# A two-layer graph network: the preparation of the edges in pieces, earlier due times, and an overlapped change of layers

## The chip, the cores and the metric

The kernel runs on one core of a Trainium2 chip. The metric is the device time of one execution in microseconds; three timed runs of the kernel before gave 4433.56, 4440.64 and 4442.63, so its median is 4440.64. The engines are called as in the profile: PE (matmuls), DVE (vector work), ACT (activations and copies from PSUM), POOL (GpSimd, which here does some vector work and issues every indirect DMA), SP (issues plain DMAs). PEld is PE's loading of weights.

## The reference

The input has 12,500 nodes of 128 features and 412,500 edges that are sorted by their destination. Two layers follow each other. Each normalises the nodes, applies relu, sums the neighbours' messages, and adds the result to x:

```python
h = jnp.maximum(_layernorm(x, axis=-1), 0.0)
# layer 0: Xs = h[src]; one of two weights by the edge's type; out = relu(segment_sum(msg, dst) + h @ W_self.T + b_self)
x = x + _L0_gnn_ref(h, edge_index, edge_type_2, ...)
h = jnp.maximum(_layernorm(x, axis=-1), 0.0)
# layer 1: agg = segment_sum((h @ W_in.T)[src], dst); deg = edges per node; out = agg + deg * (h @ W_out.T)
x = x + _L1_gnn_ref(h, ..., src, dst)
```

As the weights act on sums as well as on single messages, the kernel sums rows of h first and multiplies the sums by the weights afterwards.

## The kernel before

**Tiling.** The nodes make 98 blocks of 128, and a duo is two blocks. The normalised rows are kept as three bf16 pieces (384 columns together, high, middle and lowest), once in SBUF (`tab`) and once in DRAM (`tables[0]`, `tables[1]`), which is what is called the table. There are 33 edge tiles of 128 edges to a block.

**Two ways of summing.** In each layer some blocks (56 in layer 0, 38 in layer 1) are *gathered*: for each edge tile POOL fetches 128 rows of the table by an indirect DMA (line 580), five tiles make a group, the rows go into a ring of three groups, DVE makes a one-hot matrix (line 1130), and PE adds the tiles up (line 667). The other blocks (42 and 60) are *dense*: POOL fetches a list of edges (line 565) out of `pk`, a packed copy of the edges in DRAM; DVE unpacks it (line 1154), PE turns it, DVE marks rows and columns (lines 1142 and 1144), PE multiplies the marks to a part of an adjacency matrix (line 720), ACT copies it out (line 961), and PE multiplies it by all 98 blocks of `tab` (line 737, some six per step). ACT copies the sums out (line 899). In layer 0 a dense block has two such passes, one for each edge type, so there are 84 passes (60 in layer 1).

**Plan.** The class `Plan` (lines 66 to 146) gives each layer a row of steps, 16 to a dense pass: 1360 in layer 0, 976 in layer 1. Each engine's program is written out in the order of these steps. A group of gathered tiles has a due step, at which PE adds it up; the due steps spread evenly between step 8 and 12 steps ahead of the last dense pass's end. The blocks end one by one (self product, bias, relu, residual, and in layer 0 the next normalisation) as their sums become complete, at the earliest nine steps apart in layer 0 and four in layer 1. The end of a block of layer 0 stores a row of `tables[1]` (line 442, SP's queue) and one of x1.

**Between the layers.** When all 98 ends are stored, POOL starts with layer 1's lists and gathers. SP waits for the same, and then reloads `tab` from `tables[1]` in seven chunks of 14 blocks (line 461).

**Preparation.** Ahead of layer 0, x is loaded in seven chunks on SP's queue (line 406); ACT first issues eight weight and bias loads, then those of the edges: source, type, destination, and destination shifted by one tile (lines 824 to 834). Per chunk DVE takes statistics (lines 1034 to 1041), ACT computes the deviation (line 852) and DVE the scales. Then per duo ACT computes the normalised rows and their bf16 high piece (lines 862, 866), POOL subtracts (line 533, the split), ACT rounds the middle piece (line 879), and DVE makes the lowest piece (line 1053). The rings between these are four duos deep. Beside that stands the edges' work: POOL adds a flag to the source (line 522, payload) and checks the sort order, tile by tile (lines 543 and 545) and over half tiles (549 and 551), in four large operations; DVE makes keys (line 1067), payload (1063), highest and lowest node of each tile (1070, 1071), the minimum of the order checks (1074, 1080), and, behind the last duo, the windows (1087 to 1093), `far` (from 1096 on, small) and the listing of edges per block (1113 and 1115, two spans). The last of this is the flag `covered` (line 1122), on which all engines choose the fast path. PE turns the edge words for lists and indices (line 629), and ACT copies them out (`take`, line 848).

**Queues.** SP's queue then stores `pk` (lines 412 to 422) and the table's chunks (426).

## Time and profile before

| | |
|---|---|
| median of three runs | 4440.64 us |
| profiled execution | 4440.43 us |
| its span | 4438.4 us, mean granted clock 0.979 |
| PE busy | 4103.0 us, 92% |
| DVE busy | 3509.9 us, 79% |
| POOL busy | 3188.3 us, 72% |
| ACT busy | 2334.0 us, 53% |
| chain that ended last | PE 53%, POOL 24%, issue 9%, DVE 8%, ACT 3% |
| costliest groups | PE line 737: 14112 of 328 ns; POOL line 580: 3126 of 951 ns |

Shares of the whole span mix stages with different limits: the preparation, two layers and the stretch between them. The rows further down are therefore taken by stage. A row of the timeline gives start, length, engine, line, operation, tiles, shape and count, and in brackets the idle time ahead of it and what ended that. "issue" means that the engine waited for nothing that the profile shows.

### The profile page before, as it was taken

What the parts mean: (1) busy time and instruction counts of PE and PEld (TensorE: products, weight loads), DVE (VectorE), ACT (ScalarE), POOL (GpSimd) and SP (SyncE); (2) the same over time, 40 slices, a digit from 0 to 9 for tenths busy, and PEclk for the clock granted to TensorE, in tenths of its full rate; (3) what the DMA queues carried; (4) which work ended last, traced back from release to release, by engine and by line L of the source; (5) the groups of instructions that cost most, each with busy time, mean ns of one, the idle gap of its engine ahead of it and who ended that gap; (6) DMA issues with size and microseconds to landing.
All of it is one profiled execution on the core that took longest, in us unless ns stands there. A gap on an engine that the chain in (4) does not pass through costs nothing.

```text
span 4438.4 us, 102927 instructions
## 1 busy us (share of the span) xinstructions
PE 4103.0 (92%) x42000; PEld 2506.4 (56%) x42000; DVE 3509.9 (79%) x8092; ACT 2334.0 (53%) x3663; POOL 3188.3 (72%) x3360
## 2 busy tenths in 40 slices
PE   0399999999999999999999996999999999999999
PEld 0255555555555555555555554566656565656665
DVE  5678777787788778778777875888888888888886
ACT  4445555555555555555555553555555555555554
POOL 4377777777777777777777775777777777777776
PEclk9599999999999999999999998999999999999999
DMA  7223333333333333333333334433333333333332
GB/s 198 73 82 91 94 88 89 93 91 90 89 90 93 90 90 92 90 92 90 91 89 92 90 89 118 124 93 91 91 93 91 91 93 91 91 91 94 90 90 78
DMA packets 289371, 417.62 MB, mean 94 GB/s; under 512 B 70913, under 2 KB 228895, under 8 KB 288895
## 3 DMA queue, kind: packets, MB, share of 16 engines
q0 software_dynamic: 160160, 338.57, 27.1%
q1 hardware_dynamic: 121784, 66.09, 5.2%
q10 hardware_dynamic: 6951, 6.30, 0.6%
q8 instruction: 336, 5.51, 0.5%
q14 instruction: 140, 1.15, 0.1%
HBM read 373.52 MB, written 37.20 MB: 93 GB/s over the span
## 4 chain that ended last, share of the span: by engine, by line
PE 53%; POOL 24%; issue 9%; DVE 8%; ACT 3%; ACTq 1%; DMA 0%; POOLq 0%; DVEq 0%; SPq 0%
PE bank_d L737 33%; POOL arena L580 23%; PE bank_g L667 10%; PE banks_m L720 8%; DVE arena L1144 1%; POOL arena L565 1%; DVE arena L1142 1%; ACT arena L961 1%; ACT arena L899 1%; DVE arena L1130 1%; ACT arena L862 1%; ACTq L824 1%; PE bank_a L694 0%; PE bank_b L703 0%; DVE tab L1053 0%
## 5 line engine op out<-in xcount | busy, mean ns | idle before, releaser
L580 POOL DMA_INDIRECT arena<-table,idx x3126 | 2971.9, 951 | 1023.3 <-issue 924.1
L737 PE MATMUL bank_d<-tab,arena 128*128 128x384 bf16 x14112 | 2696.4, 328 | 36.1 <-ACT arena L899 35.1
L961 ACT ACTIVATE arena<-banks_m 128x784 bf16<-128x784 f32 x2304 | 1912.2, 830 | 1511.4 <-PE banks_m L720 1457.3
L737 PEld LDWEIGHTS bank_d<-tab,arena 128*128 128x128 bf16 x14112 | 1196.5, 98 | 955.3 <-issue 263.6
L1142 DVE TENSOR_TENSOR arena<-iota_ps,arena 128x256 bf16<-128x256 f32 (+1 forms) x2304 | 1220.6, 530 | 335.4 <-PE banks_m L720 302.9
L1144 DVE TENSOR_TENSOR arena<-iota_ps,arena 128x392 bf16<-128x392 f32 x2304 | 1279.4, 555 | 0.0
L720 PE MATMUL banks_m<-arena 64*128 64x98 bf16 (+1 forms) x13056 | 808.1, 226 | 49.7 <-ACT arena L961 36.3
L667 PE MATMUL bank_g<-arena 128*128 128x192 bf16 (+29 forms) x12753 | 763.2, 212 | 24.8 <-DMA arena<-table,idx 23.0
L667 PEld LDWEIGHTS bank_g<-arena 128*128 128x128 bf16 x12753 | 709.7, 97 | 118.2 <-issue 27.1
L720 PEld LDWEIGHTS banks_m<-arena 64*128 64x128 bf16 x13056 | 352.2, 95 | 580.6 <-ACT arena L961 419.8
L1130 DVE TENSOR_TENSOR arena<-iota_ps,rel 128x960 bf16<-128x960 f32 (+1 forms) x626 | 592.0, 946 | 3.2
L1183 DVE TENSOR_TENSOR d_sum<-arena 128x128 f32<-128x128 f32 x144 | 42.5, 295 | 319.3 <-ACT arena L899 307.2
L565 POOL DMA_INDIRECT arena<-pk,list_at x158 | 150.1, 950 | 108.0 <-issue 74.6
L922 ACT ACTIVATE arena<-bank_a 64x128 f32<-64x128 f32 x204 | 55.5, 272 | 150.1 <-PE bank_a L686 146.9
L931 ACT ACTIVATE arena<-bank_a 128x128 f32<-128x128 f32 x196 | 54.4, 277 | 136.3 <-PE bank_a L694 132.7
L899 ACT ACTIVATE arena<-bank_d 128x384 f32<-128x384 f32 x144 | 70.8, 491 | 58.1 <-PE bank_d L737 58.1
L533 POOL TENSOR_TENSOR arena<-arena,tab 128x256 f32<-128x256 f32 x49 | 35.4, 726 | 80.5 <-ACT tab L866 75.6
L685 PE MATMUL bank_a<-ident,arena 128*128 128x128 f32 x102 | 30.4, 298 | 65.8 <-DVE arena L1177 65.8
L1201 DVE SCALAR_TENSOR_TENSOR arena<-bias,count,bank_b 128x128 f32<-128x128 f32 x98 | 33.8, 345 | 61.2 <-issue 56.7
L629 PE MATMUL banks_m<-ident,arena 128*128 128x128 f32 x30 | 6.8, 397 | 78.8 <-ACT arena L848 39.5
L1154 DVE SCALAR_TENSOR_TENSOR arena<-arena,node 128x192 f32<-128x192 int32 x158 | 64.8, 410 | 16.0 <-DMA arena<-pk,list_at 16.0
L694 PE MATMUL bank_a<-ident_b,tab 128*128 128x128 bf16 x588 | 65.0, 219 | 5.1 <-ACT arena L908 2.2
(133 smaller groups left out, 1594.6 us busy)
## 6 DMA issues: line engine op xcount, KB each, us to landing
arena<-table,idx POOLq DMA_INDIRECT x3126
table<-tab SPq DMA_DIRECT2D x7, 1344.0 KB, 5.6
table<-arena SPq DMA_DIRECT2D x98, 96.0 KB
tab<-table SPq DMA_DIRECT2D x7, 1344.0 KB, 17.1
x<-arena SPq DMA_DIRECT2D x98, 64.0 KB
arena<-x SPq DMA_DIRECT2D x98, 64.0 KB
arena<-in_x_dram SPq DMA_DIRECT2D x97, 64.0 KB
out_dram<-arena SPq DMA_DIRECT2D x97, 64.0 KB
```

The source lines that it names most:

```text
L565: pool.indirect_dma_start(out=pack[:, i % PACKS, :], out_offset=None, in_=pk, in_offset=bass.IndirectOffsetOnAxis(ap=list_at[:, m:m + 1], ...
L580: pool.indirect_dma_start(out=rows[:, g % RINGS * GROUP + t % GROUP, :], out_offset=None, in_=tables[l], in_offset=bass.IndirectOffsetOnAx ...
L667: last = pe.matmul(bank_g[p % 2][:, to:to + (c1 - c0) * y], rows[:, at, a * F:(a + 1) * F], hot[:, at, c0 * y:c1 * y], start=(a == 0 and p ...
L694: last = pe.matmul(bank_a[:, 0:P], mine[:, a * F:(a + 1) * F], ident_b[:, :], start=(a == 0), stop=(a == 2))
L720: last = pe.matmul(bank_m[hf][:, n * nc_:(n + 1) * nc_], is_row[at, s_ % MARKS, n, :], is_col[at, s_ % MARKS, n * nc_:(n + 1) * nc_], star ...
L737: last = pe.matmul(bank_d[:, 0:RW], adj[q % 2][:, b * P:(b + 1) * P], tab[:, b, :], start=(b == 0), stop=(b == NB - 1))
L899: act.activation(d_sb[:, :], bank_d[:, 0:RW], ACT.Copy).then_inc(s.dense_out, 1)
L961: act.activation((adj0, adj1)[l][q % 2].rearrange("p c (h d) -> p c h d", h=2)[:, :, :, n * j:n * j + n], banks_m[:, :, 0:n * nc_].rearran ...
L1130: dve.tensor_tensor(hot[:, at:at + n, 0:c], iota_w[:, 0:c].unsqueeze(1).to_broadcast([P, n, c]), (rel0, rel1)[l][:, ts[0]:ts[0] + n].unsqu ...
L1142: dve.tensor_tensor(is_row[:, s_ % MARKS, 0:n, :], iota_r.unsqueeze(1).to_broadcast([P, n, P]), rc[:, i % 2, 0, pr:pr + n].unsqueeze(2).to ...
L1144: dve.tensor_tensor(is_col[:, s_ % MARKS, 0:n * nc_].rearrange("p (n c) -> p n c", n=n), iota_c[l].unsqueeze(1).to_broadcast([P, n, nc_]), ...
L1154: after(dve.scalar_tensor_tensor(out=arena[:, V_AT:E_AT], in0=pack[:, k, 0:W3].bitcast(i32), scalar=node[:, m:m + 1], in1=pack[:, k, W3:2 ...
```

## The change

- The edge loads are issued by SP, between the third and the fourth chunk of x, in the order destination, type, shifted destination, source. ACT issues only the weights and biases.
- POOL's payload and its two order checks are cut into 39 pieces of two of the 26 columns, 65 instructions. They stand between the splits of duos 7 to 34, one or two pieces ahead of each.
- DVE's edge work goes into a table `jobs`: for a chunk of lowest pieces, jobs in its middle and at its end. Behind the last duo remain `far` and the second span of the listing. The payload on DVE now comes ahead of POOL's flag.
- PE's centre product comes first, ACT's copy of the indices a chunk later.
- Layer 0's table rows are reloaded by chunks: `early` holds chunks 0, 1, 2, 4 and 5, which SP reloads inside layer 0's row of ends, as soon as the blocks are stored and the last dense pass is past the chunk (`s_passed`). Chunks 3 and 6 are reloaded where all were.
- POOL fetches layer 1's first four lists before it waits for the stores.
- The due steps end 28 steps ahead of the last pass's end, where it was 12, in both layers.

```diff
-            self.due = [8 + g * (self.S - 12) // self.groups for g in range(self.groups)]
+            self.due = [8 + g * (self.S - 28) // self.groups for g in range(self.groups)]
...
+    early = {}
+    for c in range(XCH):
+        passed = 16 * plans[0].Q + -(-XB[c + 1] * 16 // NB)
+        ended = max(q for q, (step, m) in enumerate(plans[0].end) if step + 9 <= passed)
+        if all(plans[0].seq[m] <= ended for m in range(XB[c], XB[c + 1])):
+            early[c] = ended
...
+            def load_x(c):
                 n0, n1 = XB[c], min(XB[c + 1], NB - 1)
                 sp.dma_start(tab_x[:, n0:n1, 0:F],
                              x[n0 * P:n1 * P, :].rearrange("(n p) f -> p n f", p=P)).then_inc(s_x[c], 16)
+            def load_edges(a, lst):
+                sp.dma_start(raw_i[a][:, 0:FCH * P].rearrange("p (c e) -> p c e", e=P),
+                             lst[0:FCH * P * P].rearrange("(c p e) -> p c e", p=P, e=P)).then_inc(s_edges[a], 16)
+                sp.dma_start(raw_i[a][0:XTRA, FCH * P:FCH * P + P],
+                             lst[FCH * P * P:FULL * P].rearrange("(p e) -> p e", e=P)).then_inc(s_edges[a], 16)
+                if REM:
+                    sp.dma_start(raw_i[a][XTRA:XTRA + 1, FCH * P:FCH * P + REM],
+                                 lst[FULL * P:E].rearrange("(p e) -> p e", p=1)).then_inc(s_edges[a], 16)
+            for c in range(3):
+                load_x(c)
+            sp.wait_ge(s_pads, 4)
+            load_edges(0, dst)
+            load_edges(1, etype)
...
+            load_edges(2, src)
+            for c in range(3, XCH):
+                load_x(c)
...
+            def reload(c):
+                sp.dma_start(tab[:, XB[c]:XB[c + 1], :],
...
+                    for c in early:
+                        if l == 0 and early[c] == q:
+                            for k in range(2):
+                                sp.wait_ge(s_stored[0][k], 32 * ((q + 2 - k) // 2))
+                            sp.wait_ge(s_passed, list(early).index(c) + 1)
+                            reload(c)
...
-            pool.wait_ge(s_edges[2], PIECES)
-            pool.tensor_scalar(raw[2], raw_i[2], float(VALID), None, op0=ALU.add).then_inc(s_pay, 1)
...
+            def piece(i):
+                a, b = i % PCS * 2, min(i % PCS * 2 + 2, CH)
+                if i < PCS:
+                    if i == 0:
+                        pool.wait_ge(s_edges[0], PIECES)
+                        pool.wait_ge(s_edges[3], PIECES)
+                    pool.tensor_tensor(steps[:, a:b, 0:P - 1], dst_i[:, a:b, 1:P], dst_i[:, a:b, 0:P - 1],
+                                       op=ALU.subtract).then_inc(s_order, 1)
+                    pool.tensor_tensor(steps[:, a:b, P - 1], nxt_t[:, a:b, 0], dst_i[:, a:b, P - 1],
+                                       op=ALU.subtract).then_inc(s_order, 1)
+                elif i < 2 * PCS:
+                    if i == PCS:
+                        pool.wait_ge(s_pay, 1)
+                    pool.tensor_scalar(pay_t[:, a:b, :], pay_t[:, a:b, :], float(VALID), None, op0=ALU.add).then_inc(s_pay, 1)
+                else:
+                    if i == 2 * PCS:
+                        pool.wait_ge(s_order, 2 * PCS + 1)
+                    pool.tensor_tensor(steps[:, a:b, 0:HALF], dst_i[:, a:b, HALF:P], dst_i[:, a:b, 0:HALF],
+                                       op=ALU.subtract).then_inc(s_order, 1)
+                    pool.tensor_tensor(steps[:, a:b, HALF:P], nxt_t[:, a:b, :], dst_i[:, a:b, HALF:P],
+                                       op=ALU.subtract).then_inc(s_order, 1)
-                if d == DUOS // 7:
-                    pool.wait_ge(s_edges[0], PIECES)
-                    pool.wait_ge(s_edges[3], PIECES)
-                    pool.tensor_tensor(steps[:, :, 0:P - 1], dst_i[:, :, 1:P], dst_i[:, :, 0:P - 1],
-                                       op=ALU.subtract).then_inc(s_order, 1)
-                    pool.tensor_tensor(steps[:, :, P - 1], nxt_t[:, :, 0], dst_i[:, :, P - 1],
-                                       op=ALU.subtract).then_inc(s_order, 1)
-                if d == DUOS * 3 // 7:
-                    pool.wait_ge(s_order, 3)
-                    pool.tensor_tensor(steps[:, :, 0:HALF], dst_i[:, :, HALF:P], dst_i[:, :, 0:HALF],
-                                       op=ALU.subtract).then_inc(s_order, 1)
-                    pool.tensor_tensor(steps[:, :, HALF:P], nxt_t[:, :, :], dst_i[:, :, HALF:P],
-                                       op=ALU.subtract).then_inc(s_order, 1)
+                while i < 3 * PCS and (i + 1) * (XB[5] // 2 - XB[1] // 2) <= 3 * PCS * (d + 1 - XB[1] // 2):
+                    piece(i)
+                    i += 1
                 split(d)
...
+                    pool.wait_ge(L[0].unpacked, len(plans[0].fetch))
+                    while n < PACKS:
+                        fetch(n)
+                        n += 1
...
+                    if l == 0 and q == plan.Q - 1 and any(XB[c + 1] == b + 1 for c in early):
+                        last.then_inc(s_passed, 1)
...
+            jobs = {1: ((payload,), (keys,)), 2: ((highest_of_tiles,), (lowest_of_tiles, order)), 4: ((), (order_half,)),
+                    5: ((windows,), (windows_1,)), 6: ((lambda: listing(0),), ())}
             def lowest(c):
-                for d in range(XB[c] // 2, XB[c + 1] // 2):
+                d0, d1 = XB[c] // 2, XB[c + 1] // 2
+                for d in range(d0, d1):
                     dve.wait_ge(s_mid, d + 1)
                     dve.tensor_tensor(tab[:, 2 * d:2 * d + 2, 2 * F:3 * F], rest[:, d % RING, :, :],
                                       tab[:, 2 * d:2 * d + 2, F:2 * F], op=ALU.subtract).then_inc(s_low, 1)
-
-            tiles = raw_i[0].rearrange("p (c e) -> p c e", e=P)
-            steps = lr[:, 0:CP].bitcast(i32)
+                    if c in jobs and d == (d0 + d1) // 2 - 1:
+                        for job in jobs[c][0]:
+                            job()
+                if c in jobs:
+                    for job in jobs[c][1]:
+                        job()
...
                 statistics(c)
-                if c == 0:
-                    dve.wait_ge(s_edges[1], PIECES)
-                    dve.wait_ge(s_pay, 1)
-                    after(dve.scalar_tensor_tensor(out=raw[2], in0=raw_i[1], scalar=float(TYPED), in1=raw[2],
-                                                   op0=ALU.mult, op1=ALU.add), s_pay, 2)
-                if c == 1:
-                    dve.wait_ge(s_edges[0], PIECES)
-                    dve.scalar_tensor_tensor(out=raw[1], in0=raw_i[0], scalar=2.0, in1=raw_i[1],
-                                             op0=ALU.mult, op1=ALU.add).then_inc(s_v, 1)
-                if c == 2:
-                    dve.tensor_reduce(tmax[:, :], tiles, axis=AX.X, op=ALU.max).then_inc(s_extent, 1)
-                    dve.tensor_reduce(tmin[:, :], tiles, axis=AX.X, op=ALU.min).then_inc(s_extent, 1)
-                if c == 3:
-                    dve.wait_ge(s_order, 2)
-                    after(dve.tensor_reduce(worst[:, 0:1], steps, axis=AX.X, op=ALU.min), s_order, 3)
                 scales(c)
                 if c > 0:
                     lowest(c - 1)
-                if c == 4:
-                    dve.wait_ge(s_order, 5)
-                    after(dve.tensor_reduce(worst[:, 1:2], steps, axis=AX.X, op=ALU.min), s_order, 6)
-                    dve.memset(lr[:, 0:BEFORE], -1.0).then_inc(s_before, 1)
-                    if LRW > BEFORE + CP:
-                        dve.memset(lr[:, BEFORE + CP:LRW], float(PAD_NODE)).then_inc(s_before, 1)
             lowest(XCH - 1)
```

POOL in the preparation, before: the splits of line 533 wait for ACT's high pieces and DVE's lowest ones, and four large checks stand between them.

```order
L533 TENSOR_TENSOR arena<-arena,tab 128x256 [waits s_hi] x4
L533 TENSOR_TENSOR arena<-arena,tab 128x256 [waits s_low,s_hi] x3
L543 TENSOR_TENSOR arena<-arena 128x26x127 [waits s_edges_next,s_edges_dst]
L545 TENSOR_TENSOR arena<-arena 128x26
L533 TENSOR_TENSOR arena<-arena,tab 128x256 [waits s_low,s_hi] x14
L549 TENSOR_TENSOR arena<-arena 128x26x64 [waits s_order]
L551 TENSOR_TENSOR arena<-arena 128x26x64
L533 TENSOR_TENSOR arena<-arena,tab 128x256 [waits s_low,s_hi] x28
```

The same place now; line 576 is the split, lines 591 and 593 the first check.

```order
L576 TENSOR_TENSOR arena<-arena,tab 128x256 [waits s_low,s_hi] x3
L591 TENSOR_TENSOR arena<-arena 128x2x127 [waits s_edges_next,s_edges_dst]
L593 TENSOR_TENSOR arena<-arena 128x2
L576 TENSOR_TENSOR arena<-arena,tab 128x256 [waits s_low,s_hi]
L591 TENSOR_TENSOR arena<-arena 128x2x127
L593 TENSOR_TENSOR arena<-arena 128x2
```

Each large operation became thirteen small ones, which stand between single splits.

POOL at the start of layer 1, before: line 565 fetches a list, line 580 gathers a tile, and `s_stored00` and `s_stored01` count layer 0's stores.

```order
L393 COMPARE_AND_BRANCH
L565 DMA arena<-pk,list_at 128x384 [waits s_stored01,s_stored00]
L565 DMA arena<-pk,list_at 128x384
L580 DMA arena<-table,idx 128x384 x15
L565 DMA arena<-pk,list_at 128x384
L580 DMA arena<-table,idx 128x384 [waits l1_added]
```

The same place now; line 625 fetches a list, line 644 gathers a tile.

```order
L404 COMPARE_AND_BRANCH
L625 DMA arena<-pk,list_at 128x384 [waits l0_unpacked]
L625 DMA arena<-pk,list_at 128x384 x3
L644 DMA arena<-table,idx 128x384 [waits s_stored01,s_stored00]
L644 DMA arena<-table,idx 128x384 x14
L644 DMA arena<-table,idx 128x384 [waits l1_added]
```

Four list fetches moved ahead of the wait for the stores, and wait for the unpacking of layer 0's last lists in its place.

PE at the end of layer 1, before: line 667 adds gathered tiles, the one with x3 being the last; line 737 is the dense product, six to a step; lines 694, 707 and 708 belong to the end of a block.

```order
L667 MATMUL bank_g<-arena 128x6 x3
L737 MATMUL bank_d<-tab,arena 128x384 x25
L667 MATMUL bank_g<-arena 128x2 x3
L737 MATMUL bank_d<-tab,arena 128x384 x12
L694 MATMUL bank_a<-ident_b,tab 128x128 x3
L737 MATMUL bank_d<-tab,arena 128x384 x6
L707 MATMUL bank_b<-wT,arena 128x128
L708 MATMUL bank_b<-wT,arena 128x128
L737 MATMUL bank_d<-tab,arena 128x384 x18
```

The same place now, from the last gathered tile on: line 731 adds gathered tiles, line 784 builds the adjacency, line 801 is the dense product, lines 758, 771 and 772 belong to ends.

```order
L801 MATMUL bank_d<-tab,arena 128x384 x7
L731 MATMUL bank_g<-arena 128x2 x3
L784 MATMUL banks_m<-arena 128x98 x8
L801 MATMUL bank_d<-tab,arena 128x384 x6
L784 MATMUL banks_m<-arena 128x98 x8
L801 MATMUL bank_d<-tab,arena 128x384 x6
L758 MATMUL bank_a<-ident_b,tab 128x128 x3
L784 MATMUL banks_m<-arena 128x98 x8
L801 MATMUL bank_d<-tab,arena 128x384 x6
```

Behind the last gathered tile there stood 49 dense products and no build; now the builds and 147 dense products of one and a half passes stand there.

## Rows read from the trace of the kernel before

**Rows 1.** Windows of layer 0 and of layer 1
```profile
190.93:2731.76 2540.83, 2450.71 (x22244) 1469.24 (x22244) 2001.54 (x4996) 1343.74 (x2101) 1862.85 (x1958) 0.99 0.32 90
2788.46:4438.40 1649.94, 1601.49 (x19391) 993.32 (x19389) 1359.09 (x2794) 883.41 (x1297) 1232.31 (x1298) 1.00 0.32 91
```

**Rows 2.** Chain of waits from 3000 to 3300 us, its shares by line
```profile
by line: POOL arena L580 72.8%; issue 24.3%; POOL arena L565 3.2%
```

**Rows 3.** Waits in layer 1, POOL 2760 to 3000, PE 3000 to 4300 us
```profile
POOL arena L580 <- PE bank_g L667: 4.8, 4, 2.9
PE bank_g L667 <- DMA arena<-table,idx: 20.0, 35, 1.5
```

**Rows 4.** Waits in layer 0, 300 to 2300 us
```profile
POOL arena L580 <- PE bank_g L667: 74.5, 68, 4.0
```

**Rows 5.** Timeline of the loads and of ACT's deviations
```profile
0.98 37.35 SPq L406 DMA_DIRECT2D tab<-in_x_dram  x7
12.79 1.30 PE L618 MATMUL bank_g<-ident,arena 128*128 128x128 f32 x5 [12.79 <-DMA bias<-in_L_gnn_b_self_dram]
33.88 8.33 ACTq L831 DMA_DIRECT2D arena<-in_dst_dram  x1
44.78 0.30 ACT L852 ACTIVATE arena<-arena,cells 128x14 f32<-128x14 f32 x1
49.77 0.30 ACT L852 ACTIVATE arena<-arena,cells 128x14 f32<-128x14 f32 x1 [1.55 <-DVE arena L1041]
124.20 0.30 ACT L852 ACTIVATE arena<-arena,cells 128x14 f32<-128x14 f32 x1 [4.75 <-DVE arena L1041]
139.59 0.31 ACT L852 ACTIVATE arena<-arena,cells 128x14 f32<-128x14 f32 x1 [4.43 <-DVE arena L1041]
```

**Rows 6.** Timeline, one lowest piece and one split
```profile
57.72 0.69 DVE L1053 TENSOR_TENSOR tab<-arena,tab 128x256 bf16<-128x256 f32 x1 [0.84 <-ACT tab L879]
86.70 0.67 POOL L533 TENSOR_TENSOR arena<-arena,tab 128x256 f32<-128x256 f32 x1 [5.58 <-ACT tab L866]
```

**Rows 7.** Timeline of DVE's tail behind the last duo
```profile
164.73 0.99 DVE L1087 TENSOR_SCALAR arena<-arena 128x3234 int16<-128x3234 int16 x1
172.63 1.84 DVE L1093 TENSOR_SCALAR idx<-idx 128x3234 int32<-128x3234 int32 x1
182.85 2.71 DVE L1113 TENSOR_TENSOR arena<-arena,node 128x2450 f32<-128x2450 f32 x1
188.93 0.15 DVE L1122 TENSOR_SCALAR covered<-bank_b 1x1 int32<-1x1 f32 x1
```

**Rows 8.** Timeline of the payload, the order checks and their neighbours
```profile
20.60 8.65 POOL L522 TENSOR_SCALAR arena<-arena 128x3328 f32<-128x3328 int32 x1 [16.36 <-DMA arena<-in_src_dram]
58.09 5.87 POOL L543 TENSOR_TENSOR arena<-arena 128x3302 int32<-128x3302 int32 x1
59.25 5.41 DVE L1053 TENSOR_TENSOR tab<-arena,tab 128x256 bf16<-128x256 f32 x2 [0.84 <-ACT tab L879]
93.42 3.88 POOL L549 TENSOR_TENSOR arena<-arena 128x1664 int32<-128x1664 int32 x1
```

**Rows 9.** Windows, a stretch with stores on SP's queue
```profile
50.00:55.00 5.00, 1.56 (x8) 1.56 (x9) 4.93 (x5) 4.91 (x15) 3.20 (x3) 1.00 1.20 314
```

**Rows 10.** Timeline between the layers
```profile
2740.50 0.35 SPq L442 DMA_DIRECT2D table<-arena  x1
2747.08 0.33 SPq L442 DMA_DIRECT2D table<-arena  x1
2750.47 0.95 POOL L565 DMA_INDIRECT arena<-pk,list_at  x1 [33.41 <-DMA x<-arena]
2758.02 0.42 DVE L1154 SCALAR_TENSOR_TENSOR arena<-arena,node 128x192 f32<-128x192 int32 x1 [10.96 <-DMA arena<-pk,list_at]
```

**Rows 11.** Timeline of the end of layer 1
```profile
4401.30 0.64 PE L667 MATMUL bank_g<-arena 128*128 128x78 bf16 x15
4416.24 0.95 POOL L580 DMA_INDIRECT arena<-table,idx  x1 [0.30 <-issue]
```

More of the change, by code:

```diff
@@ L59, in gnn_kernel @@
     XCH = 7
+    PCS = -(-CH // 2)
     XB = [NB * c // XCH // 2 * 2 if c < XCH else NB for c in range(XCH + 1)]
@@ L403, in _ @@
             sp.wait_ge(s_x_pad, 1)
-            for c in range(XCH):
+            def load_x(c):
                 n0, n1 = XB[c], min(XB[c + 1], NB - 1)
@@ L1048, in scales, with keys, payload @@
                                                op0=ALU.mult, op1=ALU.mult), s_shift, 2 * c + 2)
+            tiles = raw_i[0].rearrange("p (c e) -> p c e", e=P)
+            steps = lr[:, 0:CP].bitcast(i32)
+            GR = -(-CH // 4)
+            def keys():
+                dve.wait_ge(s_edges[0], PIECES)
+                dve.scalar_tensor_tensor(out=raw[1], in0=raw_i[0], scalar=2.0, in1=raw_i[1],
+                                         op0=ALU.mult, op1=ALU.add).then_inc(s_v, 1)
+            def payload():
+                dve.wait_ge(s_edges[1], PIECES)
+                dve.wait_ge(s_edges[2], PIECES)
+                after(dve.scalar_tensor_tensor(out=raw[2], in0=raw_i[1], scalar=float(TYPED), in1=raw_i[2],
+                                               op0=ALU.mult, op1=ALU.add), s_pay, 1)
@@ new lines, in listing @@
+            def listing(k):
+                a, n = SPANS[k]
+                if k == 0:
+                    dve.wait_ge(s_trc, 2 + 3 * GR)
+                    dve.wait_ge(s_packed, 16 * 6)
+                seen = lr[:, a:a + NB * TPB].rearrange("p (m t) -> p m t", t=TPB)[:, :, 0:n]
+                less = raw[0][:, 0:NB * TPB].rearrange("p (m t) -> p m t", t=TPB)[:, :, 0:n]
+                after(dve.tensor_tensor(less, seen, node[:, :].unsqueeze(2).to_broadcast([P, NB, n]), op=ALU.is_lt),
+                      s_lists, 2 * k + 1)
+                after(dve.tensor_reduce(before[:, k, :], less, axis=AX.X, op=ALU.add), s_lists, 2 * k + 2)
@@ L1106, in _ @@
                                      op0=ALU.is_lt, op1=ALU.add).then_inc(s_missed, 1)
[L1108 to L1115 removed]
+            for k in range(1, len(SPANS)):
+                listing(k)
             for k in range(1, len(SPANS)):
```

86 lines of the change are left out of this document (43 added, 43 removed).

## The prediction

> **What bounds the kernel now.** I read the share of each engine first, then the windows of the two layers, then the chain of waits, then the timeline of the three places that the change touches.
>
> Layer 0 takes 2541 us and layer 1 1650 us from its first dense matmul on [rows 1]; ahead of the one stand 191 us of preparation, between them lie 57. The reader is to see that PE is busy 96 to 97% of both layers, which alone would say that PE bounds both. The waits say otherwise for layer 1: the chain there consists of POOL's gathers, their issue time and its list fetches [rows 2]; POOL waited for PE 4.8 us in all, in the layer's first 240 us, and after that PE waited for gathers 35 times, 20.0 us [rows 3]. In layer 0 it is the other way: POOL waited for PE 68 times in 2000 us, 74.5 us [rows 4]. So an earlier due time should be free in layer 0, and in layer 1 it is paid at the end.
>
> In the first stage one deviation (ACT line 852) per chunk of 14 blocks marks the beat. The first is at 44.78 us [rows 5], though the weights were in at 12.79: ACT stood issuing edge loads until 33.88 + 8.33 = 42.2. The last two beats, with no edge job on DVE between them, are 139.59 - 124.20 = 15.39 us apart. The beat is a chain: of one duo DVE's lowest piece takes 0.69 us and then idles 0.84 for ACT's next, 1.53 in all [rows 6]. DVE's tail after the last duo goes from 164.73 to 189.08, 24.35 us [rows 7].
>
> **Prologue.** The first deviation now waits for weights (12.79), their transposes and two small ACT steps; I put it at 15.5. Two beats were 4.99 apart at the start [rows 5], five later ones cost 15.39 each: 15.5 + 5.0 + 77.0 = 97.5 for the beginning of chunk 6. DVE carries five edge jobs in those chunks, each one pass over 3,328 elements. The two passes over 3,234 elements between lines 1087 and 1093 took (172.63 - 165.72) / 2 = 3.5 each [rows 7], so one of these 3.6: 18.0, in series, 115.5 (before 139.59). From there to the last duo were 164.73 - 139.59 = 25.1. The listing and window jobs now also stand there. The span from 164.73 to 182.85 held them and the small far operations [rows 7]. I take windows_1 (3.5 + 1.8 = 5.3) in full because it stands at a chunk's end, and 4 us of the 11.6 placed in the middle of a chunk, as the other engines fill their rings of four while DVE is away, and DVE catches up 0.84 us per duo: 34.4, so 149.9. Of the tail remain listing 1 to the flag, 189.08 - 182.85 = 6.2, and the small far operations, 1.4 (182.85 - 174.47 less two passes of 3.5): 157.5.
>
> POOL's pieces come on top. A check over 3,302 elements took 5.87 us, a thirteenth of which is 0.45; a split of 256 elements took 0.67, which at the check's 1.78 ns each is 0.46 of work and 0.21 fixed [rows 6, 8]. Thirteen pieces each: the first check 0.45 + 0.21 + 0.21 for its two columns; the payload 8.65 / 13 + 0.21 = 0.88; the second check two of 3.88 / 13 + 0.21 = 0.51. That is 13 x (0.87 + 0.88 + 1.02) = 36.0 us. Between two splits POOL has 1.53 - 0.67 = 0.86 free, 28 duos give 24.1, and 11.9 stay over: I take X = 12. Bounds: 0, if the idle time at each chunk's start takes the rest; 30, if a piece can't run beside DVE's lowest either (28 x 0.69 less cover, 6.7 left, 29.3). For this last the trace speaks: two lowest pieces, 1.38 by themselves, took 5.41 beside the 5.87 us check [rows 8]. I stay near the lower half, since there DVE stood at a single long operation, and a short one finds the 0.84 us in which DVE waits anyway. The Trainium skill, "SBUF — State Buffer", section "Who interferes with whom", says that a DVE operation with two SBUF inputs and a GpSimd operation shut each other out completely; the 5.41 agrees, and by that rule X would be at its upper bound and the gain here about 2. It speaks against the edit that cuts the work in pieces, as cutting doesn't lessen the lock.
>
> Flag before 189.08, after 157.5 + 12 = 169.5: **-19.6** (bounds -32 and -2). The edge loads cost nothing in the sum: on SP's queue they take DMA time that the x chunks took earlier, and stores went through that queue alone at 314 GB/s [rows 9]. Behind them on that queue wait x's chunks 3 to 6 and the stores of `pk`; statistics need chunk 3 at about 51 (15.5 + 5.0 + 2 x 15.4), and the 9.4 MB ahead of its end take 30 us at that rate. Centre and index copies were moved off ACT's and PE's early path; both have slack there.
>
> **Transition.** The last block's table row is stored at 2747.08 because block 55's end stands before it, stored at 2740.50; POOL's first list fetch follows 3.39 later, at 2750.47 [rows 10]. With due times 16 steps earlier blocks 54 and 55 end before the last dense block does, and the last end follows that directly: -6.58. Against it, one more end than before falls ahead of the last dense matmul, 1.6 by my estimate (one turn, one own product and a step's wait): **-5.0** (-6.6 to -2). The reload by chunks was 0 on the path: SP's waiting loads lie beside the first build, and dense work started without a wait. Its five early chunks only move DMA into layer 0's end. I cost it 0 (-3 to +3).
>
> **Layer 1.** From 2750.47 to the last gather at 4416.24 are 1665.8 us [rows 10, 11]. Less the 4.8 of waits [rows 3], 1325 intervals (1266 gathers and 60 lists) give 1.2536 each: 0.95 and 0.30 of issue, as the row of the last gather shows. Four lists now come before the stores: -5.0. The 4.8 of waits go too, because PE has its lists at once (10.96 us of waiting for them [rows 10]). So the last gather starts 1656.0 after the stores, and lands and is marked some 4.2 later: 1660.2. PE then has steps 952 to 988 left. Before, the group due at 953 was added at 4401.30 [rows 11], and the span ended at 4438.4: 37.1, less three later groups' matmuls, 1.3 to 1.8, plus one step of 1.37 = 36.5 (a step is 1650 / 1000 with its share of groups, less without). End: 1696.7 after the stores, against 4438.4 - 2750.47 = 1687.9: **+8.8**, bounds 0 and +24 (the 16 steps in full).
>
> Layer 0's due shift: 0, as POOL's 1958 gathers and lists x 1.2536 = 2455 are well below its 2541; upper bound +10.
>
> Sum: -19.6 - 5.0 + 8.8 = -15.8, span 4422.6. The run lay 2.0 above its span (4440.43 and 4438.4), and within 0.2 of the median: **4424.6 us**. Written by X, it is 4412.6 + X.
>
> **Rivals.**
> (B) Layer 1 isn't bound by POOL. PE's 97% speaks for it. Then the lists' 10.96 count in full and the shift is free: 4424.6 - 8.8 - 11 = 4405. Against it: after 3000 us POOL waited for nothing but its own issue.
> (C) One queue is slower than two for the loads. The x chunks on SP's queue alone took 37.35 us to issue for 6.4 MB, 172 GB/s [rows 5]; the 5.8 MB of edges behind the first three chunks at that rate land at about 54. The payload job stands at about 42 (15.5 + 5.0 + 15.4, and four duos of 1.53): 12 late, 4436.6, no change by measure. Against it is [rows 9]. The Trainium skill, "DMA: Bandwidth & Descriptors", section "Issuing engines are not separate DMA queues", says that all transfers share the same 16 engines whichever engine starts them; by that, C is wrong and the move costs nothing.
> (D) Slower: the pieces block the chain duo by duo. If each of the 65 instructions, however small, costs what a split does, 0.67 us [rows 6], and none finds cover because DVE's lowest and POOL shut each other out, X = 43.6, and the time is 4456. It is slower than before by the measure from X = 37 on, 0.57 per instruction. For it speaks the 5.41 [rows 8]; against it, that the check's own price per element leaves 0.21 for the rest.
> (E) Layer 0 becomes bound by gathers. PE had 16 steps more for the same gathers; at +10 the time is 4434.
>
> **How the numbers follow.** Forecast 0.58 (own range 4412 to 4432), B 0.09, C 0.13, D 0.10, E 0.10. The range to hold 8 in 10 leaves out B's lower end and D: 4402 to 4444. A measurement of this kernel tells 0.2%, 8.9 us, from no change: faster is below 4431.8, slower above 4449.5. Faster: 0.56 of the forecast's chance, 0.09 of B's, 0.03 of C's, 0.04 of E's = 0.72. Slower: D's and a remnant of C's, 0.11. Same: 0.17.
>
> **What would show it.** First deviation at about 15.5, the one of chunk 6 near 120 to 128; the flag near 169.5. POOL's piece rows: 0.2 to 0.6 us each, and the idle time of DVE's lowest unchanged at 0.8; if lowest rows stretch, the lock is at work. SP's loads of edges landed before 45 us. First list fetches of layer 1 before the last store, its first gather about 3.4 us behind that store. POOL without waits for PE in layer 1, and more time of PE's waits for gathers than 20.0. From the last gather to the end 40 us where 22.2 were. I am wrong if layer 1 takes less time from its first gather to the end than 1691 us, or if the flag comes after 187.

## The result and the profile after

The changed kernel takes 4411.82 us (median of four runs, 4410.71 to 4412.21) against 4440.16 of the kernel before in the same runs: a ratio of 0.9936, 95% interval 0.9924 to 0.9949. It is 28 us faster; 16 were forecast. The profiled execution has a span of 4408.9 us (4438.4 before).

The same cuts through both traces, in us. The flag is the end of `covered`; "gather" is POOL's first indirect DMA of layer 1 behind the wait for the stores (in the kernel before a list fetch); "eviction" is ACT's copy of layer 0's last dense sums.

| stretch | before | after | difference | forecast |
|---|---|---|---|---|
| start to flag | 189.08 | 151.71 | -37.4 | -19.6 |
| flag to eviction | 2542.68 | 2540.34 | -2.3 | +1.6 |
| eviction to gather | 18.71 | 19.25 | +0.5 | -6.6 |
| gather to last gather | 1665.77 | 1652.88 | -12.9 | -9.8 |
| last gather to end | 22.16 | 44.72 | +22.6 | +18.5 |
| span | 4438.4 | 4408.9 | -29.5 | -15.8 |

(The forecast's -5.0 for the transition stands here as +1.6 and -6.6, its +8.8 for layer 1 as -9.8 and +18.5, rounded.)

The timeline of ACT's deviations (line 902 now), which answers to [rows 5]. The columns are start, length, engine, line, operation, shapes, count, and idle time ahead with its releaser:

```profile
14.36 0.31 ACT L902 ACTIVATE arena<-arena,cells 128x14 f32<-128x14 f32 x1
19.36 0.31 ACT L902 ACTIVATE arena<-arena,cells 128x14 f32<-128x14 f32 x1 [1.55 <-DVE arena L1091]
35.37 0.31 ACT L902 ACTIVATE arena<-arena,cells 128x14 f32<-128x14 f32 x1 [5.05 <-DVE arena L1091]
56.66 0.31 ACT L902 ACTIVATE arena<-arena,cells 128x14 f32<-128x14 f32 x1 [7.96 <-DVE arena L1091]
78.97 0.31 ACT L902 ACTIVATE arena<-arena,cells 128x14 f32<-128x14 f32 x1 [8.01 <-DVE arena L1091]
94.83 0.31 ACT L902 ACTIVATE arena<-arena,cells 128x14 f32<-128x14 f32 x1 [4.89 <-DVE arena L1091]
113.94 0.31 ACT L902 ACTIVATE arena<-arena,cells 128x14 f32<-128x14 f32 x1 [4.48 <-DVE arena L1091]
...
142.80 1.43 DVE L1163 TENSOR_TENSOR tab<-arena,tab 128x256 bf16<-128x256 f32 x4
...
151.56 0.15 DVE L1200 TENSOR_SCALAR covered<-bank_b 1x1 int32<-1x1 f32 x1
```

The first deviation is at 14.36, where 44.78 stood. The first gap between deviations is 5.0 us, as before; the five behind it are 16.0, 21.3, 22.3, 15.9 and 19.1 us; the undisturbed one before was 15.39. The reader is to look at the second gap, 19.36 to 35.37, and the fifth, 78.97 to 94.83: both hold pieces on POOL and no job on DVE, and they are 0.6 and 0.5 over a gap with neither. The third, fourth and sixth hold pieces too, and two, three and one of DVE's jobs. These five together are 17.6 over five undisturbed gaps.

POOL's first piece, which stands in the second gap, and what POOL's splits (line 576) waited for from 30 to 106 us (total, times, longest):

```profile
30.79 0.61 POOL L591 TENSOR_TENSOR arena<-arena 128x254 int32<-128x254 int32 x1 [3.08 <-DMA arena<-in_dst_dram]
```

```profile
POOL arena L576 <- ACT tab L916: 15.4, 4, 8.9
```

The first piece waited 3.1 us for the load of the edges. The four waits are those of the first split behind each deviation, so from the first piece to the last (30.79 to 105.04) POOL still had 15.4 us of idle time.

Between the layers, in answer to [rows 10]:

```profile
2687.55 4.66 SPq L491 DMA_DIRECT2D tab<-table  x1
2692.05 0.49 ACT L949 ACTIVATE arena<-bank_d 128x384 f32<-128x384 f32 x1 [6.44 <-PE bank_d L801]
2692.26 4.50 SPq L478 DMA_DIRECT2D table<-arena  x1
...
2700.36 0.29 DVE L1304 TENSOR_TENSOR arena<-arena 128x128 bf16<-128x128 f32 x1 [0.44 <-ACT arena L1004]
2702.22 0.39 SPq L491 DMA_DIRECT2D tab<-table  x1
2702.66 1.49 SPq L478 DMA_DIRECT2D table<-arena  x1
...
2711.30 0.94 POOL L644 DMA_INDIRECT arena<-table,idx  x1 [52.80 <-DMA x<-arena]
```

Line 478 stores a block's table row, line 491 reloads a chunk. The store behind three reloads took 4.50 us to issue (0.33 in [rows 10]); it is that of the last row but one. The last row of the table was ready at 2700.65, its store was issued 2.0 later behind another reload, and POOL's gather came 8.64 behind that issue, where 3.39 lay between the two before. That reload held SP itself: in its program SP waits there until the rows of the last end but one are stored (line 480 stores the row of x1), and only then come the reload and the last store. SP's waits from 2660 to 2715 show it:

```profile
SPq L491 <- DMA x<-arena: 4.9, 1, 4.9
```

Layer 1, in answer to [rows 2, 3, 4, 11]: the chain of 3000 to 3300, PE's waits for gathers from 3000 to 4300 (total, times, longest), POOL's waits for PE in layer 0 from 300 to 2300, and the end of the layer.

```profile
by line: POOL arena L644 72.3%; issue 24.4%; POOL arena L625 3.5%
```

```profile
PE bank_g L731 <- DMA arena<-table,idx: 32.8, 51, 1.5
```

```profile
POOL arena L644 <- PE bank_g L731: 54.0, 56, 3.2
```

```profile
4359.50 0.52 PE L731 MATMUL bank_g<-arena 128*128 128x42 bf16 x15 [0.35 <-DMA arena<-table,idx]
4364.18 0.95 POOL L644 DMA_INDIRECT arena<-table,idx  x1 [0.30 <-issue]
4366.06 0.52 PE L731 MATMUL bank_g<-arena 128*128 128x22 bf16 x15
4372.05 0.22 PE L731 MATMUL bank_g<-arena 128*128 128x2 bf16 x3
```

The chain is the same as before, POOL's gathers. PE waits for them 32.8 us in place of 20.0, and from the last gather on 44.7 us of PE's steps follow. Layer 0 still has POOL waiting for PE, 54.0 us in place of 74.5.

### The profile page after: what moved, and what is told of

It reads as the page before. It is cut to its first block, busy times and chain, and to the rows that moved or that the text cites. A ratio compares the mean times of both kernels' runs of the same rounds, so it can differ in the third digit from the quotient of the medians.

```text
span 4408.9 us, 102987 instructions
## 1 busy us (share of the span) xinstructions
PE 4104.2 (93%) x42000; PEld 2505.6 (57%) x42000; DVE 3502.7 (79%) x8092; ACT 2331.3 (53%) x3660; POOL 3200.3 (73%) x3420
## 4 chain that ended last, share of the span: by engine, by line
PE 52%; POOL 28%; issue 11%; DVE 5%; ACT 3%; SPq 1%; DMA 1%; POOLq 0%; DVEq 0%; ACTq 0%
PE bank_d L801 31%; POOL arena L644 26%; PE bank_g L731 10%; PE banks_m L784 8%; POOL arena L625 1%; ACT arena L1011 1%; DVE arena L1222 1%; ACT arena L949 1%; DVE arena L1220 1%; DVE arena L1208 1%; PE bank_b L767 0%; PE bank_b L769 0%; PE bank_b L768 0%; PE bank_a L758 0%; POOL arena L576 0%
## 5 line engine op out<-in xcount | busy, mean ns | idle before, releaser
L731 PE MATMUL bank_g<-arena 128*128 128x192 bf16 (+29 forms) x12753 | 764.0, 212 | 44.5 <-DMA arena<-table,idx 42.3
L1261 DVE TENSOR_TENSOR d_sum<-arena 128x128 f32<-128x128 f32 x144 | 42.3, 294 | 319.9 <-ACT arena L949 319.8
L749 PE MATMUL bank_a<-ident,arena 128*128 128x128 f32 x102 | 30.1, 295 | 41.3 <-DVE arena L1255 41.3
L758 PEld LDWEIGHTS bank_a<-ident_b,tab 128*128 128x128 bf16 x588 | 46.6, 98 | 29.5 <-issue 5.8
```

Of the source, the lines that this page charges most:

```text
L731: last = pe.matmul(bank_g[p % 2][:, to:to + (c1 - c0) * y], rows[:, at, a * F:(a + 1) * F], hot[:, at, c0 * y:c1 * y], start=(a == 0 and p ...
L758: last = pe.matmul(bank_a[:, 0:P], mine[:, a * F:(a + 1) * F], ident_b[:, :], start=(a == 0), stop=(a == 2))
```

## The experiments

Eleven kernels ran. All are the changed kernel with an edit, save one, which is the kernel before with an edit. Their stages, by the cuts of the table above (flag; flag to eviction; eviction to gather; gather to last gather; last gather to end; span):

| run | flag | layer 0 | transition | gathers | tail | span |
|---|---|---|---|---|---|---|
| before | 189.1 | 2542.7 | 18.7 | 1665.8 | 22.2 | 4438.4 |
| after | 151.7 | 2540.3 | 19.3 | 1652.9 | 44.7 | 4408.9 |
| edge loads on ACT | 181.8 | 2540.8 | 18.5 | 1654.4 | 44.4 | 4440.0 |
| edge loads alone (of before) | 178.3 | 2542.1 | 18.9 | 1664.0 | 22.6 | 4425.9 |
| POOL's work whole | 165.1 | 2540.7 | 18.3 | 1653.2 | 44.5 | 4421.7 |
| one-column pieces | 159.1 | 2538.4 | 18.7 | 1653.5 | 44.7 | 4414.4 |
| no early reload | 152.0 | 2538.4 | 12.1 | 1657.2 | 44.5 | 4404.2 |
| lists late | 152.3 | 2540.7 | 18.2 | 1661.1 | 44.6 | 4416.8 |
| layer 1 at 12 | 152.1 | 2541.2 | 18.0 | 1657.9 | 21.9 | 4391.1 |
| both: no early reload, layer 1 at 12 | 152.2 | 2541.6 | 12.0 | 1653.4 | 22.4 | 4381.6 |
| both, layer 0 at 12 too | 150.9 | 2542.6 | 18.7 | 1654.4 | 22.6 | 4389.1 |
| both, layer 1 at 8 | 152.2 | 2542.4 | 12.1 | 1653.0 | 19.5 | 4379.1 |
| both, layer 1 at 4 | 152.3 | 2537.9 | 12.0 | 1654.2 | 16.8 | 4373.1 |

Layer 0's length scatters over 5 us in kernels that do not differ in it, so differences of that size there are not read.

**Edge loads on ACT again.**

```diff
-            load_edges(0, dst)
-            load_edges(1, etype)
...
-            load_edges(2, src)
...
+            act.wait_ge(s_pads, 4)
+            for a, lst in ((2, src), (1, etype), (0, dst)):
+                act.dma_start(raw_i[a][:, 0:FCH * P].rearrange("p (c e) -> p c e", e=P),
...
```

> The changed kernel with the edge loads back on ACT's queue, ahead of its first activation, as in the kernel before; all else as changed. Changed: 4411.8 us, first deviation 14.36, flag 151.7, against 44.78 and 189.1 before. Theory: 30.4 of the 37.4 us that the flag came earlier are the start of the beat alone, as ACT no longer issues loads; then the first deviation comes at about 44.8, the flag at 178 to 183, and the time is 4438 to 4443. Rival: most of the gain is the new places of DVE's jobs and POOL's pieces, which now hide in idle time; then a late start only uses up idle time, the flag comes at 160 to 168 and the time is 4420 to 4428.

4443.46 us, ratio to before 1.0005 (0.9996 to 1.0015): the whole gain is gone. The first deviation is at 44.83, the flag is at 181.8. The gaps are the changed kernel's to within 0.1 us, save the second: it is 15.40 in place of 16.0, with the same pieces in it, and POOL does not wait for a load there. So the 0.6 of the second gap was the wait for the load, and its pieces cost nothing. The early start is worth 30.1 us; the new places of jobs and pieces are worth the other 7.3, which layer 1's longer tail takes back here.

**Edge loads alone.** The kernel before, with the loads taken out of ACT's program and put on SP's queue in their old order, between the third and the fourth chunk of x:

```diff
-            for c in range(XCH):
+            for c in range(3):
...
+            sp.wait_ge(s_pads, 4)
+            for a, lst in ((2, src), (1, etype), (0, dst)):
+                sp.dma_start(raw_i[a][:, 0:FCH * P].rearrange("p (c e) -> p c e", e=P),
...
+            for c in range(3, XCH):
```

> The kernel before with one edit: the edge loads on SP's queue between the third and fourth chunk of x, in their old order (source, type, destination, shifted destination). The changed kernel with this edit undone lost 31.6 us, so it is needed; this run asks if it is enough. Theory: it is not. In the kernel before POOL's payload stands ahead of its first operations, and DVE's payload job ahead of the first chunk's scales; both wait for source and type, so the first scales come at 33 to 40 us in place of 45.2, the flag 5 to 12 us earlier than 189.1, time 4429 to 4436. Rival: the move alone is worth the 30.4 of the first deviation: 4407 to 4412.

4424.46 us, ratio 0.9975 (0.9964 to 0.9985), flag at 178.3: 10.8 earlier, not 30. The flag is where it was expected; the time is below the expected 4429 to 4436, as that of the kernel before was 4 us lower in these runs (4436.85). The timeline of its start:

```profile
14.52 0.31 ACT L856 ACTIVATE arena<-arena,cells 128x14 f32<-128x14 f32 x1
21.88 8.65 POOL L542 TENSOR_SCALAR arena<-arena 128x3328 f32<-128x3328 int32 x1 [17.65 <-DMA arena<-in_src_dram]
30.67 3.62 DVE L1067 SCALAR_TENSOR_TENSOR arena<-arena 128x3328 f32<-128x3328 int32 x1 [20.28 <-POOL arena L542]
34.33 0.24 DVE L1050 RECIPROCAL arena<-arena 128x14 f32<-128x14 f32 x1
```

The deviation is as early as in the changed kernel, but the scales (line 1050) stand behind DVE's payload job, and that behind POOL's payload. The move and the new order of the jobs need each other: one alone gives 11 us, the other alone 7, together 37.

**POOL's work whole.**

```diff
-    PCS = -(-CH // 2)
+    PCS = 1
...
-                a, b = i % PCS * 2, min(i % PCS * 2 + 2, CH)
+                a, b = 0, CH
```

> The changed kernel with POOL's payload and its two order checks whole again (five large operations: ahead of the splits of duos 16, 25 and 34), all else as changed. Theory: the pieces cost the beat nothing (a beat with pieces and no DVE job took 15.86, 15.39 without either), because each fits in the 0.86 us between two splits, and a large one stops the splits for its whole length less what the ring of four duos covers; whole, they cost 8 to 18 us of their 23: flag at 160 to 170, time 4420 to 4430. Rival: what counts is the lock between POOL and DVE, and cutting does not lessen it; then the time stays within 3 us of 4411.8.

4427.95 us, ratio 0.9971 (0.996 to 0.9982), flag 13.3 later than in the changed kernel. Its timeline, POOL (line 591 the first check, 598 the payload) and DVE (line 1106 keys, 1163 lowest pieces):

```profile
46.81 5.86 POOL L591 TENSOR_TENSOR arena<-arena 128x3302 int32<-128x3302 int32 x1
47.05 9.11 DVE L1106 SCALAR_TENSOR_TENSOR arena<-arena 128x3328 f32<-128x3328 int32 x1
...
86.19 8.81 POOL L598 TENSOR_SCALAR arena<-arena 128x3328 f32<-128x3328 f32 x1
87.34 7.82 DVE L1163 TENSOR_TENSOR tab<-arena,tab 128x256 bf16<-128x256 f32 x2 [0.84 <-ACT tab L929]
```

and the same neighbours in the changed kernel, where line 1112 is DVE's payload job:

```profile
40.64 0.79 POOL L591 TENSOR_TENSOR arena<-arena 128x254 int32<-128x254 int32 x1
40.89 4.03 DVE L1112 SCALAR_TENSOR_TENSOR arena<-arena 128x3328 f32<-128x3328 int32 x1
41.39 3.58 POOL L593 TENSOR_TENSOR arena<-arena 128x2 int32<-128x2 int32 x1
...
49.08 3.62 DVE L1106 SCALAR_TENSOR_TENSOR arena<-arena 128x3328 f32<-128x3328 int32 x1
49.17 3.99 POOL L591 TENSOR_TENSOR arena<-arena 128x254 int32<-128x254 int32 x1
```

The lock between the two engines is there in both. Whichever started first ran on, and the other waited. With large operations DVE's keys took 9.11 us in place of 3.62; with pieces DVE loses at most one piece in these rows (4.03 for 3.6), and it is POOL's two-column operation that takes 3.58 for 0.19. Cutting the work of the engine that isn't on the path turned round who waits. The lock does not hold for every pair: DVE's reductions, which read one input, took 3.61 us beside pieces that kept their 0.84 (from 61.94 on in the changed kernel).

Not all of the 13.3 is shown to be the lock. The third gap is 3.8 longer (25.1), and that is the lock alone, as POOL had no split to do behind its check. The fifth and the sixth gap are 5.3 and 4.5 longer, and there the splits stood behind POOL's large operation as well; the run does not part the two. The fourth gap holds three of DVE's jobs here and no work of POOL's but splits. It is 22.6, against 22.3 with pieces in it, so the pieces cost nothing there either.

**One-column pieces.**

```diff
-    PCS = -(-CH // 2)
+    PCS = CH
...
-                a, b = i % PCS * 2, min(i % PCS * 2 + 2, CH)
+                a, b = i % PCS, i % PCS + 1
```

> The changed kernel with POOL's pieces one column long in place of two: the same work in 78 pieces of 130 instructions. Theory: the pieces' time per duo (0.78 us from start to start of a two-column one) nearly fills the 0.86 us between two splits; 65 more instructions of some 0.15 to 0.2 us fixed price overfill it by 0.3 us a duo, and 4 to 12 us reach the flag: 4415 to 4424. Rival: POOL has other idle time, beside DVE's jobs and at the chunks' starts, and takes them for nothing: within 3 us of 4411.8.

4416.65 us, ratio 0.9958 (0.9944 to 0.9972), flag 7.4 later. The eight kernels with the changed kernel's preparation, itself included, have their flags between 150.9 and 152.3, so this is clear of the scatter. The fifth gap is 17.3 (82.79 to 100.11) in place of 15.9. From start to start the pieces took 51.7 us of POOL in place of 40.8, and ACT waited for POOL's splits six times, 6.7 us, in the pieces' stretch, where it had waited once, 2.2. So the two-column pieces stood near the edge of what fits: they were nearly free, and half that size is not.

**No early reload.**

```diff
-        if all(plans[0].seq[m] <= ended for m in range(XB[c], XB[c + 1])):
+        if False:
```

> The changed kernel with no chunk reloaded early: all seven are reloaded after the stores, as before. In the changed kernel the first gather of layer 1 came 19.2 us after the last dense eviction of layer 0, where 12.1 were forecast; the last store was issued 2.0 us late and landed 7.9 after its issue, where 2.7 before. Theory: the reloads of five chunks stand ahead of the last stores on SP's queue and in the DMA engines; without them the first gather comes 12 to 14 after the eviction, and as gathers bound layer 1 all of that reaches the end: 4405 to 4408. Rival: the stores are late for another reason, and a late reload holds up the first dense passes: 4411 to 4418.

4408.34 us, ratio 0.9928 (0.9912 to 0.9945). Its transition:

```profile
2690.41 0.49 ACT L949 ACTIVATE arena<-bank_d 128x384 f32<-128x384 f32 x1 [6.44 <-PE bank_d L801]
...
2698.72 0.29 DVE L1304 TENSOR_TENSOR arena<-arena 128x128 bf16<-128x128 f32 x1 [0.45 <-ACT arena L1004]
2699.03 0.33 SPq L478 DMA_DIRECT2D table<-arena  x1
2699.41 0.43 SPq L480 DMA_DIRECT2D x<-arena  x1
2701.78 6.10 SPq L491 DMA_DIRECT2D tab<-table  x3
2702.48 0.95 POOL L644 DMA_INDIRECT arena<-table,idx  x1 [45.61 <-DMA x<-arena]
```

The store is issued as soon as the row is ready, takes 0.33, and the gather follows 3.45 behind it: 12.07 from the eviction, against 19.25. Of these 7.2 us 2.0 are the late issue and 5.2 the longer way from the issue to the gather. Whether the latter is the order in SP's queue or the reloads' transfers themselves no run parts. Of the 7.2 us 4.7 show in the span, since this run's gathers were 0.3% slower each (1657.2 for 1652.9) and its layer 0 was 1.9 shorter, both within the scatter. The times alone do not tell this run from the changed kernel, as the two intervals overlap; the transition does: it is 12.0 to 12.1 in three more kernels without the early reload, and 18.0 to 19.3 in the six with it.

**Layer 1's due steps at 12.**

```diff
-            self.due = [8 + g * (self.S - 28) // self.groups for g in range(self.groups)]
+            self.due = [8 + g * (self.S - (28, 12)[l]) // self.groups for g in range(self.groups)]
```

> The changed kernel with layer 1's due steps ending 12 steps ahead of the last pass's end again; layer 0's stay at 28. From the last gather to the end the changed kernel takes 44.7 us, the kernel before 22.2. Theory: layer 1 is bound by POOL's gathers, which stay where they are, and only the steps behind the last one count: 44.7 goes to 22 to 28, time 4389 to 4396. Rival: PE bounds layer 1 (97% busy), the due steps only decide where it waits: within 3 us of 4411.8.

4392.68 us, ratio 0.9893 (0.9877 to 0.991), 19 us faster than the changed kernel. The last gather and the last added tile, to be set beside those after:

```profile
4369.18 0.95 POOL L644 DMA_INDIRECT arena<-table,idx  x1 [0.30 <-issue]
```

```profile
4370.65 0.52 PE L731 MATMUL bank_g<-arena 128*128 128x22 bf16 x15
...
4375.08 0.22 PE L731 MATMUL bank_g<-arena 128*128 128x2 bf16 x3
```

From the last gather to the end of the span at 4391.1 are 21.9 us in place of 44.7. The rival, that PE bounds the layer, falls. The waits in this run, from layer 1's first gather on:

```profile
PE bank_g L731 <- DMA arena<-table,idx: 27.1, 40, 3.1
POOL arena L644 <- PE bank_g L731: 0.9, 3, 0.3
```

Beside its busy share of 96 to 97% PE waits for gathers 27.1 us in this run and 42.3 in the changed kernel (its whole layer 1, not only 3000 to 4300), and POOL waits for PE 0.9 and 0.3.

**Lists late.**

```diff
-                    pool.wait_ge(L[0].unpacked, len(plans[0].fetch))
-                    while n < PACKS:
-                        fetch(n)
-                        n += 1
```

> The changed kernel without the early fetch: layer 1's first four lists are fetched after the stores. Theory: four of POOL's intervals of 1.25 us come back, and POOL waits for PE some 4.8 us at the layer's start as before, since PE gets its lists 11 us after the stores: 4417 to 4422. Rival: only the 5.0 of the fetches count, or less, if PE catches up while groups queue in the ring: 4411 to 4416.

4420.8 us, ratio 0.9964 (0.995 to 0.9978). The stretch of the gathers is 8.2 longer: 5.0 for four intervals, and POOL waits for PE again. In layer 1's waits (total, times, longest; line 640 gathers and line 727 adds in this kernel):

```profile
POOL arena L640 <- PE bank_g L727: 3.8, 4, 2.9
```

**Both edits together, and layer 0 at 12 as well.** The first has the two edits above (no early reload, layer 1 at 12); the second has `(12, 12)` in the same place.

> The changed kernel with no chunk reloaded early and with layer 1's due steps ending 12 steps ahead of the end. Alone the first gave 4408.3 (first gather 12.07 us after the last eviction in place of 19.25), the second 4392.7. Theory: the two act at different places, the start and the end of a layer that gathers bound, and add: 4384 to 4390. Rival: with the due steps at 12 layer 1 is bound by PE, which then waits for the late chunks: 4391 to 4396.

> As the run with both edits beside it (no early reload, layer 1 at 12), and layer 0's due steps at 12 as well, as before. Theory: the last block's end then waits for block 55's again, so the last store comes 6.6 us later after the last eviction, less the 1.6 that one more end ahead of it costs: 4 to 7 us slower than its neighbour. Rival: layer 0 pays for the earlier due steps in waits for gathers; then it is equal or up to 5 faster.

4382.89 us, ratio 0.9878 (0.9862 to 0.9894), and 4391.13, ratio 0.9897 (0.9881 to 0.9914). The first is a little under what was expected: the two edits add, and the tail is 22.4. The second shows what the due steps of layer 0 are for: at 12 the transition is 18.7 again, 6.7 longer (4 to 7 were expected, the times differ by 8.2), as two ends stand in each other's way; layer 0 itself is the same within its scatter, so it pays nothing for the earlier due steps.

**Layer 1 at 8 and at 4,** as the first of these otherwise:

> The kernel with no early reload and layer 1's due steps at 12 (4382.9 us, 22.4 from the last gather to the end), with 8 in place of 12. Theory: the last gather stays and four steps of 1.37 less stand behind it, but two ends of gathered blocks now stand with the last dense block's, one each side: 2 to 5 us faster, 4378 to 4381. Rival: the ends behind the last dense pass take the whole gain: 4382 to 4386.

> As the run beside it, with 4. Now both ends of gathered blocks precede that of the last dense block, four steps apart and behind the last dense product, where a step holds no dense work. Theory: those ends cost about what the steps saved, equal to the run with 8 within 3 us. Rival: behind the last dense product steps cost nothing, 5 us faster than with 8.

4379.08 us, ratio 0.9869 (0.9853 to 0.9886), and 4377.53, ratio 0.9871 (0.9855 to 0.9888). The tails are 19.5 and 16.8, 2.8 us for each four steps. The times lie within each other's scatter (4374.91 to 4381.86 for the last), as was expected, though the last tail is 2.7 shorter; both are some 30 us faster than the changed kernel and 58 faster than the one before.

## Why the prediction was right, and where its sizes were off

**The direction and most places were right.** Four terms lie where they were put: a large gain in the prologue, a loss at layer 1's end from the due steps, nothing in layer 0, and the lists' 5 us and POOL's 4.8 of waits. The transition's gain did not come. The forecast was 16 us, the measured gain 28; 4411.8 is just below the forecast's own range, 4412 to 4432, and inside the wide one.

**Prologue, -19.6 forecast, -37.4 measured.** The start of the beat was right (15.5, measured 14.36; worth 30.1). Two steps were sized too large. The first is "28 duos give 24.1, and 11.9 stay over: I take X = 12" for POOL's pieces. Their price was near the forecast: from start to start they took 40.8 us of POOL, 34.0 without what the lock added to two rows (3.58 and 3.99), where I had 36.0. What failed is the 24.1, as POOL has more idle time than that between the splits of a duo: with all pieces done it still had 15.4 us, ahead of the first splits behind the deviations. That is the lower bound that I named, "0, if the idle time at each chunk's start takes the rest". In the gaps X is nearly zero where rows can tell: nothing in the second and the fourth, 0.5 in the fifth. In the third and the sixth no run parts pieces from jobs.

The upper bound came from the lock, and there the reading failed, not the rule: the Trainium skill, "SBUF — State Buffer", section "Who interferes with whom", says that the lock is exclusive and that issue order decides which engine blocks. The rows agree (9.11 and 7.82 for DVE behind whole operations, 3.58 for POOL behind a job of DVE's). From "shut each other out" I concluded that cutting doesn't lessen the lock; but cutting bounds what DVE can lose to one piece. The whole operations cost 13.3 us; that this is near the 12 that I charged to the pieces is chance. (The bound's own sum is off by little: 28 x 0.69 leaves 4.8 of the 24.1 and not 6.7.)

The second is DVE's jobs. I counted five in the beats, and there are six (payload, keys, highest, lowest and two of the order), 21.6 in series; 16.5 of that showed (5.9, 6.9 and 3.7 over the undisturbed gap). That those in a chunk's middle are partly hidden fits the fourth gap of the run with POOL's work whole, where three jobs of 3.6 each cost 7.2 with no piece beside them. That the five and the 18.0 came near the measured is luck. Behind chunk 6's deviation the last duo was done after 30.3 us and not 34.4, as more of the work in the chunks' middles hid than the share I took.

**Transition, -5.0 forecast, and about -1.8 measured** (+0.5 to the gather, -2.3 before the eviction, the latter within layer 0's scatter). The step that failed is "The reload by chunks was 0 on the path ... I cost it 0 (-3 to +3)". I had looked at what waits for the reload, and not at what is queued behind it: the last stores stand on the same queue, and SP waits ahead of a reload for the stores of the end before. Without it the transition was 12.07, which is the forecast's 12.1 (18.7 - 6.6).

**Layer 1, +8.8 forecast, +9.7 measured.** The gathers' stretch was 1652.9 (1656.0 forecast). The 3.1 between them are luck: an interval was 1.2512 here and 1.2536 in the kernel before, and it scatters as much between kernels that do not differ in their gathers (1.2512 to 1.2550). The tail was 44.7 (40.7): the last group, of a single tile, is due four steps behind the one before it, and PE came to it 7.9 us after the last gather's start, where I had put 4.2. The 36.5 for steps 952 to 988 were 36.9, and the forecast's own terms give 36.7 to 37.2.

**Rivals.** B fell: PE is not the bound of layer 1. C fell: the issue of the edge loads ended at 33.2, and DVE's payload job began at 40.89, right behind the lowest piece ahead of it. Only POOL's first piece was late, by 3.1 us, of which 0.6 reached the beat. (C's own 54 is too late: 8.5 MB at 172 GB/s take 50 us.) D fell, but not on the price: the 65 instructions took 0.63 us each from start to start, near its 0.67. What failed is that none finds cover. Even in one-column form the pieces cost only 7.4 more. E fell: POOL waited for PE 54.0 us in layer 0 still.

In sum: X was 12 too high, the stretch behind chunk 6's deviation 4 and the first deviation 1, all on the side of too slow; the reload cost 6 to 7 that were not in the sum.

## What to carry to other kernels

When two engines shut each other out, cut the work of the one that isn't on the path into pieces, and add up their price from start to start against all the idle time of their engine in that stretch, not only that of one place: at 40.8 us they were nearly free, with 15.4 left idle; at 51.7, with twice the count, 7.4 reached the flag. Before moving a transfer earlier, list what is queued behind it and what its queue waits for ahead of it, not only who waits for it. A busy share of 97% doesn't name the bound: in a layer that gathers bound, putting the adds of the gathered tiles earlier in PE's order does not bring the last gather forward, and only lengthens the tail that follows it.

## What the runs showed of the hardware

A 96 KB store that was issued behind three reloads of 1344 KB on the same queue took 4.50 us to issue, against 0.33 alone. The next such store, behind one more reload, took 1.49, and its consumer started 8.64 us after the issue in place of 3.4. The interval of one gather, 0.95 us and 0.30 of issue, differed by 0.3% from run to run of the same program part (1.2512 to 1.2550 over 1321 intervals), which is 5 us of layer 1; no run here shows why. A DVE operation of two inputs over 3328 elements, 3.62 us alone, took 9.11 when a POOL operation of 5.86 had begun 0.24 ahead of it; DVE's reductions of one input, 3.61, and POOL's pieces did not lengthen each other.
